# Eight gathers and the one-hot matmuls of the last tile: the tail and the start of a routed layer, reordered

## The reference, cut to what matters

```python
def _L3_ffn_ref(hidden_states, Wr, br, Wg, Wu, Wd):     # 4 experts, 1024 hidden
    logits = x @ Wr + br
    probs = jax.nn.softmax(logits, axis=-1)
    top_w, top_idx = jax.lax.top_k(probs, 1)            # one expert per token
    g = jnp.einsum('td,edf->tef', x, Wg)
    u = jnp.einsum('td,edf->tef', x, Wu)
    h = jax.nn.silu(g) * u
    y = jnp.einsum('tef,efd->ted', h, Wd)
    sel = jnp.take_along_axis(y, top_idx[:, :, None], axis=1)[:, 0]
    return sel * top_w
...
x = x + jnp.tanh(g_ffn[3]) * _L3_ffn_ref(_layernorm(x, axis=-1), ...)
```

## Time and profile before

| | |
|---|---|
| runs shown | 1167.1, 1162.4, 1166.57 us; median 1166.57 |
| the profiled execution | 1167.27 us, its span 1165.4 us |
| busy in the span | PE 81%, DVE 58%, ACT 38%, POOL 34% |
| last routed layer, from the last logits to the end | 995.3 to 1165.4 us |

### The profile page before, as it was taken

The page is one execution under the profiler, slowest core; times in us unless marked ns, Lnnn a source line. Parts: engine busy times, 40 slices in busy tenths (PEclk is TensorE's granted clock), DMA queues, the critical chain, the costliest instruction groups (busy, mean ns, idle before and its releaser), DMA issues. The chain is left out here.

```text
span 1165.4 us, 19018 instructions
## 1 busy us (share of the span) xinstructions
PE 944.7 (81%) x6654; PEld 557.1 (48%) x6654; DVE 670.2 (58%) x1616; ACT 439.4 (38%) x726; POOL 396.6 (34%) x529
## 2 busy tenths in 40 slices
PE   3899995879189999787689726899999998399992
PEld 2455544778044456565357512344544444155652
DVE  5778753452678433677573359888887842311111
ACT  1456662211056412454114300556656575022220
POOL 5233303332632003333025250556566565100002
PEclk9999995999589999898599956899999998599997
DMA  6434424674533003744318730101210000720002
GB/s 185 125 104 148 156 106 180 195 270 158 148 108 99 1 1 69 223 104 96 132 56 232 167 97 18 41 2 43 110 47 7 6 7 10 301 73 24 15 12 81
DMA packets 109819, 115.27 MB, mean 99 GB/s; under 512 B 58696, under 2 KB 98952, under 8 KB 106696
## 3 DMA queue, kind: packets, MB, share of 16 engines
q1 hardware_dynamic: 104064, 98.72, 27.3%
q0 software_dynamic: 3936, 10.75, 4.0%
q10 hardware_dynamic: 1728, 4.59, 1.1%
HBM read 88.17 MB, written 29.62 MB: 101 GB/s over the span
## 5 line engine op out<-in xcount | busy, mean ns | idle before, releaser
L1993 DVE TENSOR_REDUCE mxp<-psB 128x1 f32<-128x512 f32 x256 | 163.4, 684 | 30.4 <-PE psB L1387 28.8
L1423 PE MATMUL psT<-whole 99*128 99x256 bf16 (+2 forms) x1024 | 154.0, 276 | 11.0 <-issue 10.6
L1997 DVE TENSOR_REDUCE mxp<-psB 128x2 f32<-128x512 f32 x192 | 123.1, 684 | 26.8 <-PE psB L1393 26.3
L1743 ACT ACTIVATE Pt<-psT,ln 128x1024 f32<-128x1024 f32 x96 | 106.1, 1114 | 59.5 <-PE psT L1423 58.8
L1423 PEld LDWEIGHTS psT<-whole 99*128 99x128 bf16 (+2 forms) x1024 | 96.2, 102 | 58.1 <-issue 28.3
L1743 ACT ACTIVATE Pt<-psT 128x1024 f32<-128x1024 f32 x96 | 98.0, 1024 | 59.4 <-PE psT L1423 57.7
L2396 POOL TENSOR_TENSOR rstd<-vare,cst 128x1 f32<-128x1 f32 x64 | 36.2, 566 | 232.9 <-DVE vare L1894 232.7
L1387 PE MATMUL psB<-whole 96*128 96x512 bf16 x256 | 91.6, 410 | 25.3 <-DVE mxp L1993 12.9
L1393 PE MATMUL psB<-whole 96*128 96x256 bf16 x384 | 75.7, 301 | 34.4 <-DMA whole<-scr_q 20.8
L2469 POOL DMA_INDIRECT xn<-scr_tokens,token x42 | 40.0, 952 | 129.4 <-PE psB L1559 56.2
L2455 POOL TENSOR_SCALAR nb_t<-Pt 128x1024 f16<-128x1024 f32 x64 | 67.2, 1050 | 44.8 <-ACT Pt L1743 43.0
(11 more groups left out here) (353 smaller groups left out, 1748.0 us busy)
## 6 DMA issues: line engine op xcount, KB each, us to landing
whole<-in_w SPq DMA_DIRECT2D x32, 512.0 KB, 5.3
whole<-in_w SPq DMA_DIRECT2D x5, 3072.0 KB, 10.5
scr_q<-sq SPq DMA_DIRECT2D x48, 96.0 KB, 2.2
whole<-scr_q SPq DMA_DIRECT2D x24, 192.0 KB
whole<-scr_k SPq DMA_DIRECT2D x24, 192.0 KB
scr_sorted_out<-xn SPq DMA_DIRECT2D x31, 128.0 KB
scr_k<-sk SPq DMA_DIRECT2D x32, 96.0 KB, 1.9
whole<-scr_k SPq DMA_DIRECT2D x24, 128.0 KB
```

The costliest lines, as they stand in the source:

```text
L1423: ins = pe.matmul(psT[:, s.n % 2, i * A.T:(i + 1) * A.T], lhsT=k_at[:, h * kw + s.c * P:h * kw + (s.c + 1) * P], rhs=q_at[:, h * A.T:(h + ...
L1743: act.activation(p_slot(A, s.p)[:, 0:4 * A.T], psT[:, s.n % 2, 0:4 * A.T], ACT.Exp, bias=bias, scale=scale).then_inc(T_used[s.n % 2], 1)
L1993: dve.tensor_reduce(mxp[:, s.un.g % 2, at:at + 1], psB[:, s.n % BANKS, :], AX.X, ALU.max).then_inc(bank_used[s.n % BANKS], 1)
L1997: dve.tensor_reduce(mxp[:, s.un.g % 2, at:at + 2], psB[:, s.n % BANKS, :].rearrange("p (h n) -> p h n", h=2), AX.X, ALU.max).then_inc(bank ...
```

## The change

It has four parts.

1. **Routing.** The one-hot and its sums move to a zeroed piece of `tmp` (`sums`, eight blocks of zeros ahead of eight of data), and the eight additions in sequence become three of 32 columns each (distances 1, 2, 4). ScalarE's exponentials go to `cm`, and what DVE makes of them (denominator, reciprocal, gate) goes to a new step `pick3` after tile 2's second half. The table `te` is made after `token`.
2. **Load.** SP waits for tile 0's gather before it issues `w14`.
3. **Early gathers.** The eight `gather3` wait for ten tiles, 0 to 9, and for `pick3`, and no longer for the last. `pick3` also makes a gate that is zero for tokens of the last tile (`r8[:, 4]`), the places with zero for these (`idx[:, 1]`), and a one-hot `slot_last3` of slot by token for the last tile; `turn3`, after tile 4's second half, turns it on PE into `pick3` (the tensor). The last tile's order on PE is now `su(10,0)`, `sh(9,1)`, `sd(9)`, `su(10,1)`, `sh(10,0)`, `sh(10,1)`, `sd(10)`, and it is not stored.
4. **Last tile by matmul.** Eight matmuls (`last3`) bring the last tile's rows to the blocks; DVE adds each to `x`. The additions of blocks 0 to 3's gathers (`EARLY3` = 4) stand ahead of the last tile's copy on DVE, those of blocks 4 to 7 between the `last3`.

```diff
@@ sorted_experts
+        final = TILES3 - 1
         for t in range(TILES3):
             su(t, 0)
             if t >= 1:
                 sh(t - 1, 1)
             if t + 1 < TILES3:
                 sx(t + 1)
+            if t == final:
+                sd(t - 1)
+                for b in range(NB):
+                    add("gather3", b=b)
             su(t, 1)
-            if t >= 1:
+            if 1 <= t < final:
                 sd(t - 1)
+            if t == 2:
+                add("pick3")
+            if t == 4:
+                picked = add("turn3", m=take("M")).m
             sh(t, 0)
-        sh(TILES3 - 1, 1)
-        sd(TILES3 - 1)
-        for b in range(NB):
-            add("gather3", b=b)
-        for b in range(NB):
-            add("combine3", b=b)
+        sh(final, 1)
+        for b in range(EARLY3):
+            add("combine3", b=b)
+        sd(final)
+        for b in range(NB):
+            if b >= EARLY3:
+                add("combine3", b=b)
+            add("last3", b=b, m=take("M"), m_x=picked, s=tiles[final].s)
@@ SP
                 elif s.kind == "sx_load":
                     sp.wait_ge(experts_in, 32)
+                    sp.wait_ge(tile_in[0], 16 * (uses2(0) + 1))
                     sp.dma_start(whole[:, 2 * SLOTW:3 * SLOTW], t["w14"]).then_inc(experts_in, 16)
...
-                elif s.kind == "combine3":
+                elif s.kind == "last3":
                     sp.wait_ge(combined3, s.b + 1)
@@ PE
+                elif s.kind == "turn3":
+                    dst = m_begin(s.m)
+                    pe.wait_ge(picked3, 1)
+                    for b in range(NB):
+                        ins = pe.transpose(psB[:, s.m % BANKS, :].bitcast(BF16)[:, b * P:(b + 1) * P], slot_last3[:, b, :],
+                                           ident16[:, :])
+                    ins.then_inc(bank_ready[s.m % BANKS], 1)
+                elif s.kind == "last3":
+                    dst = m_begin(s.m)
+                    if s.b == 0:
+                        evacuated(pe, s.m_x)
+                        evacuated(pe, s.s)
+                    pe.matmul(dst, lhsT=pick3[:, s.b, :], rhs=so[:, (TILES3 - 1) % 4, :], start=True, stop=True
+                              ).then_inc(bank_ready[s.m % BANKS], 1)
@@ ACT
+                elif s.kind == "turn3":
+                    turn(act, bank_ready, s.m)
+                    act.activation(pick3, psB[:, s.m % BANKS, :].bitcast(BF16).rearrange("p (b n) -> p b n", b=NB), ACT.Copy
+                                   ).then_inc(bank_used[s.m % BANKS], 1)
+                elif s.kind == "sd" and s.i < TILES3 - 1:
@@ DVE, route
+                        oh3 = sums[:, 0, NB:2 * NB, :]
+                        link(dve.memset(tmp[:, 0:256], 0.0))
...
+                        first_max(L, n, oh3)
+                        for i, back in enumerate((1, 2, 4)):
+                            link(dve.tensor_tensor(sums[:, i + 1, NB:2 * NB, :], sums[:, i, NB:2 * NB, :],
+                                                   sums[:, i, NB - back:2 * NB - back, :], ALU.add))
+                        dve.sem_inc(route_pe, 1)
...
-                        link(dve.memset(rc[:, 0, 0:4], 0.0))
-                        for b in range(1, NB):
-                            link(dve.tensor_tensor(rc[:, b, 0:4], rc[:, b - 1, 0:4], oh[:, b - 1, 0:4], ALU.add))
-                        link(dve.tensor_tensor(rc[:, 0, 8:12], rc[:, NB - 1, 0:4], oh[:, NB - 1, 0:4], ALU.add))
@@ DVE, the end
                 elif s.kind == "combine3":
                     b = s.b
                     dve.wait_ge(gathered3[b], 16)
-                    dve.scalar_tensor_tensor(out=x[:, b, :], in0=gathered_x[:, b, :], scalar=r8[:, 3, b:b + 1],
-                                             in1=x[:, b, :], op0=ALU.mult, op1=ALU.add).then_inc(combined3, 1)
+                    link(dve.scalar_tensor_tensor(out=x[:, b, :], in0=gathered_x[:, b, :], scalar=r8[:, 4, b:b + 1],
+                                                  in1=x[:, b, :], op0=ALU.mult, op1=ALU.add))
+                elif s.kind == "last3":
+                    b = s.b
+                    turn(dve, bank_ready, s.m)
+                    dve.scalar_tensor_tensor(out=x[:, b, :], in0=m_slot(s.m), scalar=r8[:, 3, b:b + 1],
+                                             in1=x[:, b, :], op0=ALU.mult, op1=ALU.add).then_inc(bank_used[s.m % BANKS], 1)
+                    evacuated(dve, s.m)
+                    dve.sem_inc(combined3, 1)
@@ DVE, pick3
+                    dve.wait_ge(route_b, 4)
+                    link(dve.tensor_reduce(r8[:, 1, :], cm[:, :, 0:4], AX.X, ALU.add))
+                    link(dve.reciprocal(gate, r8[:, 1, :]))
+                    link(dve.tensor_scalar(gate, gate, tg[:, 7:8], None, ALU.mult))
+                    link(dve.tensor_scalar(early, tile_of, float(TILES3 - 1), None, ALU.is_lt))
+                    link(dve.tensor_tensor(early_gate, gate, early, ALU.mult))
+                    link(dve.tensor_tensor(early, place, early, ALU.mult))
+                    link(dve.tensor_copy(idx[:, 1, :], early))
+                    dve.tensor_tensor(slot_last3, slot_low3, slot_hit3[:, :, TILES3 - 1].unsqueeze(2).to_broadcast([P, NB, P]),
+                                      ALU.mult).then_inc(picked3, 1)
@@ POOL
                         for i in range(4):
-                            pool.wait_ge(sorted_out[i], 16 * (uses2(i) + (TILES3 - 1 - i) // 4 + 1))
+                            pool.wait_ge(sorted_out[i], 16 * (uses2(i) + (TILES3 - 2 - i) // 4 + 1))
+                        pool.wait_ge(picked3, 1)
```

49 lines of the change are left out of this document (25 added, 24 removed).

## The result

| | before | changed |
|---|---|---|
| median of the runs, us | 1165.19 (4 runs) | 1152.74 (4 runs) |
| lowest and highest | 1162.4, 1167.1 | 1147.04, 1158.13 |
| profiled execution, its span | 1167.27, 1165.4 | 1153.11, 1150.9 |

The ratio is 0.9899, with a 95% interval from 0.9864 to 0.9933: faster, by 1.0%. The changed kernel was timed a second time among the experiments: 1152.67 (6 runs), ratio 0.9898. The forecast was 1156.0, range 1152.5 to 1160.5.

What follows compares the result with a forecast made beforehand. It took a chain of small DVE steps to bound the start, PE the tiles, POOL and DMA the tail. Start 5.3 plus tail 6.4 less 0.5 gave 11.2 us off the profiled 1167.27: 1156.0, range 1152.5 to 1160.5.

Steps and rivals of the forecast that it cites:

- Start, routing and load: Last logits to first tile: first gather 2.96 us earlier and taking 2.8 in place of 5.10; tiles start 5.3 earlier.
- rival B: First gather at the start: its 5.10 us are its own, the start gains only 2.96, time 1158.5; chance 0.05.
- The table late next: Expert table made behind `token` at the start: six instructions, 1.3 us, ready at 1007.1, before the gather lands.
- The clock's rise: First half tile on PE: the low clock costs the same 2.63 us again; a rise 1.5 sooner or later is worth 0.75.
- Middle: Among the tiles: `pick3` on DVE, 2.8 us, hidden in 4.3 idle, cost 0; `turn3` on PE taken as 0.5.
- Tail, PE and the copy: Last tiles: new waits on PE start `sd(10)` 1.8 us later; the fourth gathered addition holds tile 10's copy half a microsecond.
- Tail, DVE: Behind tile 10's copy: twelve additions at 0.52 us, 6.2 in all; block 7 ends at 1155.4, 6.4 saved.
- The end: Behind the last addition: the last store and what lies behind it stay unchanged.
- Two rules weighed: Tail gathers beside DVE additions: POOL takes what it takes alone; by the skill's port lock the end would be 0.7 us later.
- A: Tail: PE's clock falls in three gaps of about 1 us, `sd(10)` takes 3.45 more, time 1159.5; chance 0.07.
- C: Early tiles: the held load makes PE wait for `w15` at tile 2, 2 to 4 us lost, 1158.1 to 1160.1; chance 0.04.
- D: Early tiles: PE stutters and its clock stays at 1.2 GHz; lasting 30 us, it gives 1168.6, slower; chance 0.03.

Runs made afterwards that it cites:

- the tail alone: Changed kernel with the old routing step and without the held load of `w14`: 1159.22 us (10 runs), ratio 0.9948.
- The run with separate banks: Changed kernel with each of the eight `last3` matmuls in a PSUM bank of its own, not a ring of three: 1151.05 us, ratio 0.9880.

## Why the prediction was right

The sum said 11.2 us less than the profiled execution of before, and from the mark on it was 10.3 in one profile and 12.9 in the other. That the first is so near is in part luck: the additions gave 1.8 less than the sum, and the end 1.0 more. Its number, 1156.0, was made against an execution of 1167.27, 2.1 us above the 1165.19 that the median of before came to; that is most of the 3.3 between forecast and result.

- *Start, routing and load*: 5.3 forecast, 5.35 measured. The parts are right too, as far as they go: the first gather was 3.07 earlier (2.96 forecast) and took 2.82 (2.8). What the text did not see is that they need each other: the 5.3 came out, but its split into 2.96 and 2.3 did not. It gave 2.96 to the routing and 2.3 to the hold, and in rival B let the routing's 2.96 stand alone. The run without the hold shows 0.3 for the routing. Rival B's price, 1158.5, was reached by that kernel (1158.87), but by way of the tail alone.
- *The table late next*: it did not show; the table was done at 1003.09, and the first up projection waits for `qf` alone, 0.62 us.
- *The clock's rise*: the same cost was forecast, and 6.24 or 5.24 stand against 6.11. A scatter of 1 us is in it.
- *Middle*: from the first half tile's end to the tail's first gather are 118.70 us against 126.54, 7.8 less; the text had the gathers 8.2 earlier and half a microsecond lost to `turn3`, 7.7. `pick3` cost nothing.
- *Tail, PE and the copy*: sum 2.3 later by `turn3` and the new gaps, then 0.5 by the fourth addition: 2.8. Measured 2.83 and 2.57 (*copy 10*).
- *Tail, DVE*: this is the term that was mis-sized. The text had 6.98 from the copy's end, with 0.52 for each addition; measured were 8.79 and 7.83. Of that 0.85 is the wait behind each addition from PSUM (0.63 in place of 0.52) and the first product, 0.86 behind the copy in place of 0.73, the two together. The form's row of layer 0 gave the addition's busy time, and not the step from one to the next. The rest, 0.96 in the first profile, is in the two gaps that the second doesn't have. The run with separate banks comes to 6.93, the number of the text, but by luck: there the additions begin 1.63 behind the copy, not 0.73, and the twelve take 5.30, not 6.24.
- *The end*: "unchanged" was wrong to the good side. 3.56 us became 2.25, since the end no longer hangs on POOL's DRAIN, 6.77 us behind its last gather. The text saw the last store there and not POOL, and counted the earlier gathers' worth for the additions alone. In the first profile this makes up for half of what the additions fell short by; in the second for more than all of it.
- *Two rules weighed*: the eight gathers took 942 to 950 ns each, four of them beside gathered additions, and came every 1.25 us. The hold that the Trainium skill (SBUF — State Buffer, "SBUF: two separate sides") gives for a VectorE operation in a two-port mode, 0.7 in the sum, does not show in this stage. The section names two-port modes apart from operations with two inputs in SBUF, which these additions are, and of the latter it says only that they and a GpSimd operation that reads SBUF hold each other; so the text's reading of 0.48 for each addition went beyond it.

The group of the gathers, in the changed kernel (ns min/median/max):

```profile
L2537 POOL DMA_INDIRECT xn_t<-scr_sorted_out,idx x8: 942/945/950, 1131.7 to 1140.5; - x8
```

The rivals: A did not come, the clock is 1.00 through stretches in which PE was busy for 1.26 of 3 us. C and D did not: no `su` waits for a load, and all of PE's waits from the first half tile on are

```profile
PE psB L1617 <- ACT ctx_t L1827: 1.8, 2, 0.9
PE psB L1596 <- DVEq L2329: 1.2, 1, 1.2
PE psB L1610 <- DVE x L2342: 1.1, 2, 0.7
PE psB L1610 <- issue: 0.9, 1, 0.9
PE psT L1589 <- ACT qf L1818: 0.6, 1, 0.6
```

(us in total, times, longest). The held load of `w14` landed as `w15` was issued, at 1017.76, 12.3 us behind its own issue where 10.3 were forecast, and that was early enough.

## What to carry to other kernels

Before a chain of small steps ahead of a transfer is shortened, ask whether the transfer's end hangs on its own start or on that of a large load beside it: here 3 us of routing were worth 0.3 until the load was held back. Price a row of small instructions by the distance from one start to the next, waits for their own writes included, not by their busy time. Look at how each engine's queue ends, and not only at the last store: here 1.3 us of the gain lay in POOL's end. Where identical code scatters more than the change is worth, measure stages from the last common mark, and profile the same kernel twice: here two stages repeated within 0.1 us, two others scattered by 1, their sum by 2.6, and medians of six runs carry 4.

## What the runs showed of the hardware

- A gather of one tile (128 rows) issued 2.8 to 5.6 us behind a load of 3 MB landed 10.6 to 10.8 us behind the load's issue in three kernels, whenever it was itself issued; with the load held back it took 2.6 to 2.8 from issue to landing, in eleven.
- Bf16 matmuls of 128x256 on idle time raised the granted clock from 0.50 to 1.00 ahead of fp32 work, which then took 3.69 and 3.70 us for eight matmuls in place of 5.1 to 6.3; in a third kernel the clock fell back to 0.50 before that work, which took 5.39. The start was not longer for it (14.91 to 14.97 us against 15.33).
- The rise of the clock in work that starts cold scattered by 1.1 us between profiles of the same instructions (5.17 to 6.31).
- DVE's copy of a PSUM bank behind four additions came 0.10 to 0.35 us or 1.19 to 1.30 behind PE's modelled end, and 0.03 to 0.05 with none ahead of it. The cause is not settled.
- POOL's DRAIN at the end of the program ended 6.77 or 6.78 us behind the end of the row in which it issued its last gather of the tail, in all fourteen profiles. In four of them it ended behind SP's and the span closed 0.23 us later.
- Stores of 128 KB took 1.7 us to land with nothing beside them and 2.6 to 2.7 beside gathers.
